# First pass of a convolution kernel: GpSimd works the taps of the fourth chunk, partial sums lie in PSUM, stores go to the sync queue

## The chip, the cores and the metric

The kernel runs on one core of one Trainium2 chip. The metric is the device time of one execution in microseconds. Three runs of the kernel before took 4022.09, 4029.52 and 4029.68 us, so the median is 4029.52. A separate execution was profiled; its own time is in the table below.

## The reference, cut to what matters

The input x is float32, 8 images of 512 channels of 128 x 128. Two branches are computed from it and joined. The part of the program at issue makes two things of x in one reading: a grouped convolution with stride 2 (two input channels to one output channel, 3 x 3 taps), and a projection of every channel's image onto 64 fixed cosine products.

```python
x = jax.lax.conv_general_dilated(sx, w_down, window_strides=(2, 2), padding=((1, 1), (1, 1)),
                                 feature_group_count=c2, dimension_numbers=('NCHW', 'OIHW', 'NCHW'))
...
xP = jnp.einsum('bcn,nk->bck', x2, P)
```

The convolution's result (8 x 256 x 64 x 64) feeds a k-means clustering, a mixture fit, a gate and a bilinear enlargement; the projection feeds an attention in the 64 coefficients. Both come back in a second pass over x. Those later passes are the same in both kernels.

## The kernel before

The program has a first pass, a cluster pass, an average pass, a mixture pass and a second pass, one after the other, with a barrier of all engines between them. Only the first pass is touched.

The first pass takes x in 16 groups: 8 images by T = 2 halves of the channels. A group is 128 partitions, each with the S = 2 input channels of one output channel. Each group is cut by rows into CH1 = 4 chunks of 32 rows. A chunk has one input buffer (`xt[c]`, 4.2 MB with one extra row above) and one accumulator (`acc[c]`, 128 x 16 x 64), so a buffer comes back into use once a group.

The convolution has 18 taps: two input channels by nine positions, each a strided window of the chunk times one weight per partition. For every chunk ScalarE writes tap 0 into the accumulator (L213) and counts `started`. VectorE adds the other 17 with one instruction each (L188): x window times weight plus accumulator, back into the accumulator. It takes chunks 0 and 1 together, one tap of each in turn, then 2 and 3. Each tap waits for the tap before it on the same chunk, by `tapped`. When a pair is done it counts `chunk_free` for each chunk. GpSimd issues the store of each accumulator to the array `downsampled` in HBM (L163), waits for it to land and counts `stored`, which ScalarE needs before it starts the same chunk of the next group.

The projection runs beside this. TensorE transposes x in quads, four 128 x 128 blocks at a time, into one of SLOTS = 4 PSUM banks (`first_tp`, L243); ScalarE copies a quad to SBUF (`first_xT`, L217); TensorE multiplies it into `first_freq` (L255) two quads behind the transposes. A group is 64 quads, 16 a chunk. At a group's end ScalarE copies the sums out (L220), TensorE folds the two halves (`first_sum`, L273) and ScalarE copies the result (L222).

The sync engine issues the loads of x in the order of chunks (L144). A load waits until TensorE has transposed the old contents (`pe_read`) and VectorE has done its taps (`chunk_free`).

The order of the work is written out by hand: each engine has its own list of instructions in a loop over images (SP and GpSimd over groups), with two groups in the loop's body, and semaphores join the lists. Engines run their lists strictly in order.

## Time and profile before

| | before |
|---|---|
| median of 3 runs | 4029.52 us |
| profiled execution | 4018.82 us |
| its span | 4017.1 us |
| first pass ends (first read of the cluster pass issued) | 1368.14 us |
| TensorE busy in the span | 3405.0 us (85%) |
| VectorE busy | 2899.9 us (72%) |
| ScalarE busy | 2079.5 us (52%) |
| GpSimd busy | 34.8 us (1%) |
| taps on VectorE, L188 | 1088, 1298.0 us busy, mean 1274 ns |
| transposes, L243, and products, L255 | 4096 each, 680.2 and 667.8 us busy |

The span runs from the first to the last instruction of the profiled execution. Busy time is the time in which an engine had at least one instruction under way; instructions overlap at their ends, so the mean of one tap (1274 ns) is more than the distance between two. PE is TensorE, PEld its weight loads, DVE VectorE, ACT ScalarE, POOL GpSimd, SP the sync engine, and a q behind an engine's name its queue. "Idle before" is how long the engine stood still before a row, and behind the arrow is what ended it; "issue" means that nothing the profile shows was waited for.

### The profile page before, as it was taken

The numbers are of one execution on the slowest core, as the hardware profiler recorded it, in microseconds if no ns is written. First come the engines' busy times: TensorE is split into PE (matmuls) and PEld (weight loads), VectorE is DVE, ScalarE is ACT, GpSimd is POOL, SyncE is SP. The second block draws the span as 40 slices with busy tenths as digits, with TensorE's granted clock in tenths as the row PEclk, the third lists the DMA queues.
The fourth block names the chain that finished last, engine by engine and source line by source line (L and its number), as shares of the span: only waits on it lengthen the run. The fifth ranks groups of instructions, "written<-read, shape, count | busy, mean of one in ns | idle before, by whom it ended". The sixth has DMA issues, their size and how long they took to land. (4 is left out here: it accounts for less than half of the span.)

```text
span 4017.1 us, 69326 instructions
## 1 busy us (share of the span) xinstructions
PE 3405.0 (85%) x24688; PEld 2542.9 (63%) x24688; DVE 2899.9 (72%) x3732; ACT 2079.5 (52%) x3496; POOL 34.8 (1%) x69
## 2 busy tenths in 40 slices
PE   7998999999999368995666898888888888888887
PEld 4454544545545266773444787878778787877877
DVE  5999999999999721114334877768677777868766
ACT  4555555555555202221112667666666666666766
POOL 0000000000000000000000000000000000000000
PEclk9999999999999668997887999999999999999999
DMA  6555565646565204210002999999899999989998
GB/s 282 227 236 246 220 262 204 267 205 261 220 246 237 81 0 167 108 70 0 0 0 91 345 316 320 318 321 323 305 333 322 330 318 322 324 314 330 315 348 284
DMA packets 348928, 945.65 MB, mean 235 GB/s; under 512 B 25938, under 2 KB 58834, under 8 KB 329491
## 3 DMA queue, kind: packets, MB, share of 16 engines
q1 hardware_dynamic: 339346, 907.41, 60.9%
q0 software_dynamic: 9216, 33.56, 2.1%
q8 instruction: 207, 3.39, 0.3%
q14 instruction: 159, 1.29, 0.1%
HBM read 638.89 MB, written 301.99 MB: 234 GB/s over the span
## 5 line engine op out<-in xcount | busy, mean ns | idle before, releaser
L188 DVE SCALAR_TENSOR_TENSOR first_acc<-first_x,first_wd,first_acc 128x1024 f32<-128x1024 f32 (+1 forms) x1088 | 1298.0, 1274 | 57.7 <-ACT first_acc L213 46.3
L1139 PE MATMUL second_o<-second_right,second_left 128*128 128x128 f32 x8192 | 1144.6, 285 | 105.6 <-ACT second_right L1220 61.9
L1139 PEld LDWEIGHTS second_o<-second_right,second_left 128*128 128x128 f32 x8192 | 1033.6, 198 | 162.0 <-issue 139.5
L1370 DVE TENSOR_TENSOR second_x<-second_o,second_x 128x512 f32<-128x512 f32 x1024 | 702.5, 689 | 465.3 <-PE second_o L1139 456.5
L217 ACT ACTIVATE first_xT<-first_tp 128x512 f32<-128x512 f32 x1024 | 609.2, 598 | 535.1 <-PE first_tp L243 534.7
L243 PE MATMUL first_tp<-all_const,first_x 128*128 128x128 f32 x4096 | 680.2, 291 | 78.7 <-issue 42.6
L243 PEld LDWEIGHTS first_tp<-all_const,first_x 128*128 128x128 f32 x4096 | 442.8, 144 | 461.0 <-issue 446.5
L255 PE MATMUL first_freq<-first_xT,all_p 128*64 128x256 f32 x4096 | 667.8, 407 | 17.5 <-ACT first_xT L217 7.8
L1192 ACT ACTIVATE second_scaled<-second_mid,second_shift,second_gain 128x512 f32<-128x512 f32 x512 | 388.6, 806 | 366.7 <-DVE second_mid L1352 338.4
L1215 ACT ACTIVATE second_left<-second_tp 64x512 f32<-64x512 f32 x512 | 302.5, 591 | 157.8 <-PE second_tp L1126 139.0
L1126 PE MATMUL second_tp<-all_const,second_scaled 128*128 128x128 f32 x2048 | 322.4, 282 | 29.1 <-ACT second_scaled L1192 29.1
L255 PEld LDWEIGHTS first_freq<-first_xT,all_p 128*64 128x64 f32 x4096 | 210.6, 136 | 193.4 <-issue 178.4
L1216 ACT ACTIVATE second_left<-second_tp 64x512 f32<-64x512 f32 x512 | 303.4, 593 | 5.9
L1126 PEld LDWEIGHTS second_tp<-all_const,second_scaled 128*128 128x128 f32 x2048 | 246.0, 145 | 44.2 <-ACT second_scaled L1192 36.2
L564 DVE TENSOR_TENSOR gates_ft<-gates_ft,average_mean 128x512 f32<-128x512 f32 x64 | 44.0, 688 | 239.8 <-PE average_mean L516 239.8
L1126 PE MATMUL second_tp<-all_const,second_zt 128*128 128x128 f32 x512 | 106.5, 291 | 121.7 <-ACT second_left L1216 121.6
L1340 DVE TENSOR_TENSOR second_part<-second_dd,all_inter 128x512 f32<-128x512 f32 x256 | 174.5, 682 | 0.0
L1340 DVE TENSOR_TENSOR second_mid<-second_dd,all_inter 128x512 f32<-128x512 f32 x256 | 174.3, 681 | 0.2 <-DVE second_rr L1321 0.2
L539 ACT ACTIVATE average_dT<-average_tp 128x512 f32<-128x512 f32 x128 | 74.9, 597 | 168.9 <-PE average_tp L494 168.9
L1352 DVE TENSOR_TENSOR second_mid<-second_mid,second_part 128x1024 f32<-128x1024 f32 x128 | 156.6, 1224 | 4.8 <-DVE second_rr L1321 1.6
L1126 PEld LDWEIGHTS second_tp<-all_const,second_zt 128*128 128x128 f32 x512 | 60.4, 144 | 139.8 <-ACT second_left L1216 137.4
L1069 PE MATMUL second_st<-second_pk,all_p 128*64 128x64 f32 x2048 | 142.8, 234 | 3.7 <-DVE second_pk L1275 3.7
(208 smaller groups left out, 2322.6 us busy)
## 6 DMA issues: line engine op xcount, KB each, us to landing
second_x<-in_x SPq DMA_DIRECT2D x512, 512.0 KB, 6.0
out<-second_x SPq DMA_DIRECT2D x512, 512.0 KB, 4.4
first_x<-in_x SPq DMA_DIRECT2D x48, 4224.0 KB, 25.3
first_x<-in_x SPq DMA_DIRECT2D x16, 4096.0 KB
second_dd<-downsampled SPq DMA_DIRECT2D x112, 384.0 KB, 5.7
downsampled<-first_acc POOLq DMA_DIRECT2D x64, 512.0 KB, 11.6
average_xd<-downsampled SPq DMA_DIRECT2D x16, 2048.0 KB, 8.6
second_dd<-downsampled SPq DMA_DIRECT2D x16, 320.0 KB, 5.5
```

What stands on the lines that cost most here:

```text
L188: nc.vector.scalar_tensor_tensor(out=acc[c][:, :, left:], in0=tap_window(xt[c], (s, dh, dw), OUT1), scalar=wd[:, t, k:k + 1], in1=acc[c][: ...
L217: nc.scalar.activation(xT[slot][:, :, :], tp[slot][:, :, :], ACT.Copy).then_inc(copied[slot], 1)
L243: last = nc.tensor.transpose(tp[slot][:, n * S + s, :], xt[c][:, s, 1 + r + n, :], ident)
L255: last = nc.tensor.matmul(freq_ps[t][n * UV:(n + 1) * UV, 0:S * P], p_sb[:, row, :], xT[slot][:, n * S:(n + 1) * S, :].rearrange("p s g -> ...
L1126: last = nc.tensor.transpose(tp[slot][:, i, :], src.rearrange("p h w -> p (h w)"), k("ident"))
L1139: last = nc.tensor.matmul(ob[n][:, r, :], left[a][:, r, n, :], right[a][:, r, :], start=True, stop=True)
L1192: last = nc.scalar.activation(scaled_rows[c][:, t, s, :, :], mid[c][:, t, :, :], ACT.Identity, scale=gain[:, n:n + 1], bias=shift[:, n:n + 1])
L1215: nc.scalar.activation(left[a][lo, 2 * n + 1, :, :], tp[slot][lo, :, :], ACT.Copy)
L1216: nc.scalar.activation(left[a][hi, 2 * n, :, :], tp[slot][hi, :, :], ACT.Copy).then_inc(copied[slot], 1)
L1340: last = nc.vector.tensor_tensor((mid[c], part)[r][:, :, :, :].rearrange("p t (i e) w -> p t i e w", e=2)[:, :, :, 1 - e, :], dd[c][:, :, ...
L1352: nc.vector.tensor_tensor(mid[c][:, :, :, :], mid[c][:, :, :, :], part[:, :, :, :], ALU.add).then_inc(interpolated, 1)
L1370: nc.vector.tensor_tensor(xt[i][:, n // S, n % S, :, :], ob[n][:, :, :], xt[i][:, n // S, n % S, :, :], ALU.add).then_inc(added[n], 1)
```

## The change

GpSimd takes the 17 taps of chunk 3 of each group. It has no instruction here that multiplies and adds at once, so each tap is a scaling into a buffer `product` and an add of it into the accumulator, both in SBUF; its list is written out for all 16 groups, without a loop. Each of the 34 instructions waits for the one before it. VectorE keeps chunks 1 and 0, one tap of each in turn, and then chunk 2 in two halves of 8 output rows, one tap of each half in turn. Its running sums lie in PSUM (`partial`): the first tap reads ScalarE's accumulator from SBUF, the last one writes it there. The order of the taps is new, so that the last covers all columns.

The two partial sums take four PSUM banks. The transposes therefore have two banks (TP_BANKS) where they had four, and the folded sums go to the free columns of `first_freq`. TensorE's transposes of quad q now wait for the copy of quad q - 2 in place of q - 4. The stores leave GpSimd and stand on the sync queue, each in front of the load of the same chunk of the next group. A load waits for `pe_read`; that the taps are done follows from the store before it, which waits for them.

On the sync engine, the loop over groups reads as follows before (`first_x` is a chunk's input, `downsampled` the array of results):

```order
L144 ISA [waits first_chunk_free2,first_pe_read2]
L144 DMA first_x<-in_x 128x2x4224
L144 ISA [waits first_chunk_free3,first_pe_read3]
L144 DMA first_x<-in_x 128x2x4224
L152 REGISTER_ALU
L152 COMPARE_AND_BRANCH
```

and now:

```order
L163 ISA [waits first_tapped2]
L163 DMA downsampled<-first_acc 128x1024
L151 ISA [waits first_pe_read2]
L151 DMA first_x<-in_x 128x2x4224
L163 ISA [waits first_tapped3]
L163 DMA downsampled<-first_acc 128x1024
L151 ISA [waits first_pe_read3]
L151 DMA first_x<-in_x 128x2x4224
L167 REGISTER_ALU
L167 COMPARE_AND_BRANCH
```

Before each load there is now a wait for the chunk's last tap and a store. On GpSimd the list of a group before is stores and waits:

```order
L163 ISA [waits first_tapped0]
L163 DMA downsampled<-first_acc 128x1024
L165 ISA
L163 ISA [waits first_xd_out0,first_tapped1]
L163 DMA downsampled<-first_acc 128x1024
```

and now (`first_product` is the scaled window, `first_wd` the weights):

```order
L190 TENSOR_SCALAR first_product<-first_x,first_wd 128x1024 [waits first_started,first_x_in3]
L194 TENSOR_TENSOR first_acc<-first_acc,first_product 128x1024 [waits first_tapped3]
L190 TENSOR_SCALAR first_product<-first_x,first_wd 128x1024 [waits first_tapped3]
L194 TENSOR_TENSOR first_acc<-first_acc,first_product 128x1024 [waits first_tapped3]
...
L190 TENSOR_SCALAR first_product<-first_x,first_wd 128x1024 [waits first_tapped3,first_started,first_x_in3]
```

The DMAs are gone from it; two arithmetic instructions a tap have come, every one with a wait for `tapped3`, and the next group's first one waits for ScalarE's start and the load as well. On TensorE the head of a group before is:

```order
L243 MATMUL first_tp<-all_const,first_x 128x128 [waits first_copied0]
L243 MATMUL first_tp<-all_const,first_x 128x128 x3
L243 MATMUL first_tp<-all_const,first_x 128x128 [waits first_copied1]
L243 MATMUL first_tp<-all_const,first_x 128x128 x3
L243 MATMUL first_tp<-all_const,first_x 128x128 [waits first_copied2]
L243 MATMUL first_tp<-all_const,first_x 128x128 x3
L251 REGISTER_ALU
L252 REGISTER_ALU [waits first_freq_read]
L255 MATMUL first_freq<-first_xT,all_p 64x256 [waits first_copied0]
```

and now:

```order
L290 MATMUL first_tp<-all_const,first_x 128x128 [waits first_copied2]
L290 MATMUL first_tp<-all_const,first_x 128x128 x3
L290 MATMUL first_tp<-all_const,first_x 128x128 [waits first_copied3]
L290 MATMUL first_tp<-all_const,first_x 128x128 x3
L287 REGISTER_ALU
L290 MATMUL first_tp<-all_const,first_x 128x128 [waits first_copied0]
L290 MATMUL first_tp<-all_const,first_x 128x128 x3
L298 REGISTER_ALU
L302 MATMUL first_freq<-first_xT,all_p 64x256 [waits first_copied0,first_freq_read]
```

Before, the three first quads waited for copies of the group before; now the third waits for the copy of this group's own first quad, as the first product does.

```diff
-TAPS = [(s, dh, dw) for dw in (0, 1) for dh in (-1, 0, 1) for s in range(S)] + \
-       [(s, dh, -1) for dh in (-1, 0, 1) for s in range(S)]
+TAPS = [(s, dh, dw) for dw in (0, -1, 1) for dh in (-1, 0, 1) for s in range(S)]
+TP_BANKS = 2
+POOL_CHUNK = 3
+STEPS = [TAPS_LEFT, TAPS_LEFT, 2 * TAPS_LEFT, 2 * TAPS_LEFT]
...
-        tp = [sc.ps(f"tp{i}", [P, 4, P]) for i in range(SLOTS)]
+        tp = [sc.ps(f"tp{i}", [P, 4, P]) for i in range(TP_BANKS)]
-        sum_ps = sc.ps("sum", [P, 512])
+        sum_ps = [bank[:, S * P:S * P + S * UV] for bank in freq_ps]
+        product = sc.sb("product", [P, OUT1, WD])
+        partial = [sc.ps(f"partial{i}", [P, OUT1, WD]) for i in range(2)]
...
                     sp.wait_ge(pe_read[c], i + FREE)
-                    sp.wait_ge(chunk_free[c], i + FREE)
...
+                def store(i, c):
+                    sp.wait_ge(tapped[c], i * STEPS[c] + STEPS[c] + FREE)
+                    sp.dma_start(xd.rearrange("b t g n -> (b t) g n")[i, :, c * OUT1 * WD:(c + 1) * OUT1 * WD],
+                                 acc[c][:, :, :].rearrange("g h w -> g (h w)")).then_inc(stored[c], 16)
+                with sp.Fori(0, B * T - 1) as i:
                     for c in range(CH1):
-                        load(i, c)
+                        store(i, c)
+                        load(i + 1, c)
...
             def _(pool):
...
+                for i in range(B * T):
+                    done = i * STEPS[c] + FREE
+                    pool.wait_ge(x_in[c], i * 16 + 16)
+                    pool.wait_ge(started, i * CH1 + c + 1)
+                    for n, (s, dh, dw) in enumerate(TAPS[1:]):
+                        left = 1 if dw < 0 else 0
+                        if n > 0 or i > 0:
+                            pool.wait_ge(tapped[c], done + 2 * n)
+                        nc.gpsimd.tensor_scalar(product[:, :, left:], tap_window(xt[c], (s, dh, dw), OUT1),
+                                                wd[:, i % T, weight_of(s, dh, dw)], None, ALU.mult
+                                                ).then_inc(tapped[c], 1)
+                        pool.wait_ge(tapped[c], done + 2 * n + 1)
+                        nc.gpsimd.tensor_tensor(acc[c][:, :, left:], acc[c][:, :, left:], product[:, :, left:],
+                                                ALU.add).then_inc(tapped[c], 1)
...
             def _(dve):
...
+                    before = acc[c] if n == 0 else mine
+                    after = acc[c] if n == TAPS_LEFT - 1 else mine
+                    return nc.vector.scalar_tensor_tensor(
+                        out=after[:, rows, left:], in0=tap_window(xt[c], (s, dh, dw), count, row0),
+                        scalar=wd[:, t, weight_of(s, dh, dw)], in1=before[:, rows, left:],
+                        op0=ALU.mult, op1=ALU.add)
...
+                        for n in range(TAPS_LEFT):
+                            for c in (1, 0):
...
+                                tap(t, c, n, slice(0, OUT1), partial[c]).then_inc(tapped[c], 1)
+                        c, half = 2, OUT1 // 2
+                        for n in range(TAPS_LEFT):
+                            for h in range(2):
...
+                                tap(t, c, n, slice(h * half, (h + 1) * half), partial[0]).then_inc(tapped[c], 1)
...
-                            pe.wait_ge(copied[slot], i * (quads // SLOTS) + q // SLOTS + FREE)
+                            before = (q - TP_BANKS) % SLOTS
+                            pe.wait_ge(copied[before], i * (quads // SLOTS) + (q - TP_BANKS) // SLOTS + 1 + FREE)
```

## Rows read from the trace of the kernel before

**Rows 1.** Timeline, all engines, end of the pass: start us, us, engine, line, work.

```profile
1355.17 0.53 POOL L163 DMA_DIRECT2D downsampled<-first_acc  x1 [36.44 <-DVE first_acc L188]
1358.78 0.53 POOL L163 DMA_DIRECT2D downsampled<-first_acc  x1 [3.08 <-DMA downsampled<-first_acc]
...
1368.14 0.82 SPq L313 DMA_DIRECT2D cluster_xx<-downsampled  x2
```

**Rows 2.** Stretch 100 to 1300 us: PE, PEld, DVE, ACT, POOL busy, clock, DMA, GB/s.

```profile
100.00:1300.00 1200.00, 1122.63 (x7560) 605.02 (x7558) 1187.35 (x996) 639.75 (x1033) 30.92 (x58) 0.97 0.58 237
```

**Rows 3.** Timeline of VectorE, two blocks of a group and the last block.

```profile
85.50 40.55 DVE L188 SCALAR_TENSOR_TENSOR first_acc<-first_x,first_wd,first_acc 128x1024 f32<-128x1024 f32 x34 [0.67 <-DVE first_acc L188]
126.40 40.55 DVE L188 SCALAR_TENSOR_TENSOR first_acc<-first_x,first_wd,first_acc 128x1024 f32<-128x1024 f32 x34 [0.34 <-DVE first_acc L188]
...
1315.15 40.55 DVE L188 SCALAR_TENSOR_TENSOR first_acc<-first_x,first_wd,first_acc 128x1024 f32<-128x1024 f32 x34 [0.23 <-DVE first_acc L188]
```

**Rows 4.** Timeline of ScalarE, starts of accumulators.

```profile
82.05 1.26 ACT L213 ACTIVATE first_acc<-first_x,first_wd 128x1024 f32<-128x1024 f32 x1
...
632.22 1.26 ACT L213 ACTIVATE first_acc<-first_x,first_wd 128x1024 f32<-128x1024 f32 x1 [1.64 <-DMA first_x<-in_x]
652.49 1.26 ACT L213 ACTIVATE first_acc<-first_x,first_wd 128x1024 f32<-128x1024 f32 x1
...
719.77 1.25 ACT L213 ACTIVATE first_acc<-first_x,first_wd 128x1024 f32<-128x1024 f32 x1
738.69 1.25 ACT L213 ACTIVATE first_acc<-first_x,first_wd 128x1024 f32<-128x1024 f32 x1
...
815.62 1.25 ACT L213 ACTIVATE first_acc<-first_x,first_wd 128x1024 f32<-128x1024 f32 x1
...
900.41 1.26 ACT L213 ACTIVATE first_acc<-first_x,first_wd 128x1024 f32<-128x1024 f32 x1
...
921.91 1.29 ACT L213 ACTIVATE first_acc<-first_x,first_wd 128x1024 f32<-128x1024 f32 x1
939.53 1.27 ACT L213 ACTIVATE first_acc<-first_x,first_wd 128x1024 f32<-128x1024 f32 x1
...
1308.86 1.27 ACT L213 ACTIVATE first_acc<-first_x,first_wd 128x1024 f32<-128x1024 f32 x1
```

**Rows 5.** Timeline of TensorE, heads of two groups and a wait for x.

```profile
514.42 2.82 PE L243 MATMUL first_tp<-all_const,first_x 128*128 128x128 f32 x12 [6.13 <-issue]
...
593.47 1.48 PE L243 MATMUL first_tp<-all_const,first_x 128*128 128x128 f32 x12
595.76 0.65 PE L255 MATMUL first_freq<-first_xT,all_p 128*64 128x256 f32 x4 [0.81 <-ACT first_xT L217]
...
632.24 0.66 PE L243 MATMUL first_tp<-all_const,first_x 128*128 128x128 f32 x4 [1.50 <-DMA first_x<-in_x]
...
633.67 1.12 PE L243 MATMUL first_tp<-all_const,first_x 128*128 128x128 f32 x4
```

**Rows 6.** The page's groups by line: out<-in xcount, busy, mean ns, idle before.

```profile
L1370 DVE TENSOR_TENSOR second_x<-second_o,second_x 128x512 f32<-128x512 f32 x1024 | 702.5, 689 | 465.3 <-PE second_o L1139 456.5
...
L1340 DVE TENSOR_TENSOR second_part<-second_dd,all_inter 128x512 f32<-128x512 f32 x256 | 174.5, 682 | 0.0
```

**Rows 7.** Groups of GpSimd, shapes apart.

```profile
L158 POOL MEMSET first_x<- 128x256 f32 x1 | 0.3, 312 | 0.3 <-POOLq L1514 0.3
L1514 POOL MEMSET const-float32-0.0<- 128x1 f32 x1 | 0.1, 99 | 0.4 <-issue 0.4
```

**Rows 8.** Line L144, loads of x issued from 120 to 130 us: ns, starts; landing.

```profile
L144 SPq DMA_DIRECT2D first_x<-in_x x2: 543/543/543, 125.1 to 126.3; - x2
...
DMA to landing us min/median/max: 15.3/20.3/25.4
```

**Rows 9.** Two short stretches, columns as in rows 2.

```profile
631.00:637.00 6.00, 4.76 (x24) 2.54 (x24) 6.00 (x6) 2.55 (x4) 0.00 (x0) 0.72 0.99 421
640.00:646.00 6.00, 6.00 (x43) 3.11 (x41) 6.00 (x6) 2.99 (x5) 0.00 (x0) 1.00 0.29 122
```

More of the change, by code:

```diff
@@ L170, in _, with tap @@
                 dve.wait_ge(top_zero, 1)
[L171 removed]
+                start_free(dve, tapped[:3])
+                def tap(t, c, n, rows, mine):
+                    s, dh, dw = TAPS[1 + n]
+                    left = 1 if dw < 0 else 0
+                    row0, count = rows.start, rows.stop - rows.start
+                    before = acc[c] if n == 0 else mine
[4 more added lines that the diff above has]
+                        op0=ALU.mult, op1=ALU.add)
```

69 lines of the change are left out of this document (31 added, 38 removed).

## The prediction

> **What bounds the kernel now.** I read the busy shares first, then a table of stretches, then the groups by line, then the order of time on VectorE, ScalarE and TensorE side by side, and last the DMA landings.
>
> The first pass ends at 1368.14, where the cluster pass issues its first read [rows 1]; nothing behind that point is touched, so the question is how far it moves. Between 100 and 1300 us VectorE is busy for 1187.35 of 1200 us, TensorE for 1122.63, GpSimd for 30.92 [rows 2]. That looks like one bound, VectorE, with a neighbour 6% behind. The order of time shows less distance. VectorE's taps run in blocks of 34 in 40.55 us, 1.193 us each, with 0.2 to 0.7 us between blocks [rows 3]: about 81.6 us for a group of four chunks. ScalarE starts the accumulator of each chunk in step with TensorE, so its rows show TensorE's pace [rows 4]: chunk 3 of the first group starts at 82.05, of the sixteenth at 1308.86, so 15 intervals of 81.8 us. A pair of groups, which is one turn of the loop, takes 163.6. Now take a stretch where no row has a wait for a DMA: chunk 3 starts at 738.69, 815.62 and 900.41, which is 76.9 us inside a pair and 84.8 across a loop end, together 161.7. The 84.8 holds a 6.13 us issue gap of TensorE at the head of its loop body, and 12 transposes in 2.82 us behind it, where the same 12 take 1.48 elsewhere [rows 5]. TensorE's own pace is therefore only 1.9 us a pair shorter than what is run today. VectorE and TensorE are bounds of nearly the same height. Unloading VectorE alone can give back about 8 x 1.9 = 15 us.
>
> **The change part by part.**
>
> VectorE. It keeps 34 full taps and 34 half taps of 68 full ones. Full: 34 x 1.193 = 40.6 us. Half: a two-input operation of 512 columns reads 682 ns [rows 6], one of 1024 columns 1274, of which 1193 count; 512 columns then count some 0.60 us, and 34 x 0.60 = 20.4. Sum 61.0 against 81.1, far below TensorE's 81. A partial sum in PSUM as input costs little by the rows: 689 ns where one input is PSUM, 682 where both are SBUF [rows 6]. No row has VectorE writing PSUM; I bound it by 0 and by 0.08 us (the whole tail of a tap, 1.274 long against 1.193 apart) and take 0.03.
>
> The Trainium skill (Perfetto Trace Analysis, "Optimizing Scalar/DVE Operations") puts the access overhead of VectorE at about 60 ns on SBUF and 125 ns on PSUM; by that estimate a tap is 0.065 us longer. No run here shows it.
>
> GpSimd. It gets 17 pairs of a scaling and an add, 34 instructions of 128x1024, each waiting for the one before, as GpSimd's rows in the section on the change show. The trace has no GpSimd arithmetic at all. The nearest rows are its memsets: 312 ns for 256 elements, 99 ns for one [rows 7], so 0.835 ns an element for one stream and 0.1 us fixed. If an instruction's streams all run beside each other, each costs 0.95 us, a pair 1.9. If they run one behind the other, the scaling (one in, one out) costs 1.81 and the add (two in, one out) 2.66, a pair 4.5. The handover from one instruction to its dependent is bounded by 0 and 0.34 us, VectorE's idle time between two blocks of a group, where it waits for its own result [rows 3]. So 17 taps take L = 32 us at least and 17 x (4.47 + 0.68) = 88 at most. Neither row is nearer than the other; I take the middle for the arithmetic, 3.19, and 0.28 for each of two handovers: 3.75 a tap, L = 63.8.
>
> The Trainium skill (GPSIMD Engine Reference, "Performance versus the Vector engine") gives 4497 ns for an fp32 add of 2048 elements; half of it with a one-input scaling at line rate would put L at an estimated 64, and its warning that ordinary elementwise work belongs on VectorE is the rule that speaks against this change. No run here shows either figure.
>
> The loop that L closes. Chunk 3 of a group can't start on GpSimd before ScalarE has started its accumulator, which ScalarE reaches only after the three chunks before it; and the x buffer of chunk 3 is reloaded only after the last add, since the store comes first on the sync queue and waits for it, as the queue's rows show there. From that add to the next start: 0.2 us to the issue (a chunk's last tap ends at 124.9, 1.2 before the block's end at 126.05 [rows 3]; the load goes at 125.1 [rows 8]), 0.6 for the store's own issue, 15.3 to landing [rows 8], 1.4 for the store that is ahead in the queue (the two loads, issued at 125.1 and 126.3, take 15.3 and 25.4, so they land 11.3 us apart, for 4.2 MB; the store is 0.5 MB), 1.3 for ScalarE's accumulator [rows 4]. Sum 18.8. The cycle is L + 18.8 = 82.6 us.
>
> TensorE with two transpose banks. Today it runs three quads of transposes at a group's head, 12 in a row, and its first product waits until 595.76 for the copy, which stands behind ScalarE's accumulator [rows 5]. Afterwards the third quad waits for that copy too (TensorE's rows there), so one quad of transposes (0.58 us) comes behind it: +0.6 inside a pair, +1.0 behind the loop end, where the clock is low. Inside a group a copy has about 1 us of slack to the transposes that need its bank, and the accumulator at a chunk's head (1.27) leaves some 0.3 of it, so I cost it at nothing there.
>
> The clock. After a wait of 1.5 us for x at 632.24, four matmuls take 1.12 us where they took 0.66 [rows 5]; the granted clock is 0.72 over 631 to 637 and 1.00 over 640 to 646 [rows 9], so the engine falls from 2.4 to 1.2 GHz for a while. A wait above 1.5 us for x costs some 1.3 us more: chunk 2 started at 632.22 and chunk 3 at 652.49, 20.27 apart, where 18.92 is usual, as 719.77 to 738.69 [rows 4]. I add 1.3 once for each such wait.
>
> Stores. They leave GpSimd's queue, where their issue and waits cost nothing today, since nothing waits for them. On the sync queue they stand ahead of the loads; the price, 0.6 + 1.4 us, is in the 18.8.
>
> **The sum.** Starts of chunk 3: 15 intervals, 8 inside a pair, 7 across. Inside, max(82.6, 76.9 + 0.6) = 82.6. Across, max(82.6, 84.8 + 1.0 + 1.3) = 87.1. From 82.05 [rows 4]: 82.05 + 8 x 82.6 + 7 x 87.1 = 1352.6, where it is 1308.86 today: +43.7. Then the tail. Today VectorE ends at 1355.70 and the next pass starts 12.4 us later, behind two stores in turn [rows 1, 3]. Afterwards GpSimd ends last, at 1352.6 + 1.3 + 63.8 = 1417.7; one store and the barrier follow, which take 9.4 today (1358.78 to 1368.14). The pass ends at 1427.1 instead of 1368.1: +59. The profiled execution took 4018.82 with a span of 4017.1; that gives 4078. The median of the three runs is 4029.52, 10.7 above the profiled one, so for a median I forecast 4088, 1.5% slower. Less than 0.2% (8 us) can't be told from no change.
>
> **Rivals.**
>
> A, GpSimd is quicker than the cycle needs (L below 59). Then TensorE sets the pace: 8 x 77.5 + 7 x 85.8 brings the last start to 1302.7, 6 us earlier than today, and the tail grows by L - 45.6 less 3. At L = 55 that is no change (about 4029), at 59 about +6. What takes the place of GpSimd is chunk 0: VectorE may begin only when ScalarE has started chunk 1 (921.91 to 939.53 and 1.3 more [rows 4], 18.9 us into the group), works 40.6, and the load lands 17.5 later: 77.0, against 77.5 when TensorE wants it. 0.03 a tap uses that up; 0.08 a tap makes 8 stalls of 2.2 + 1.3 us, +28: 4057. For it: one-input work may be quick. Against it: 34 dependent handovers.
>
> B, the other side: GpSimd's streams overlap fully, L is under 45, and taps into PSUM cost no more than today. Then TensorE's pace is reached and the tail shrinks: at L = 40 the pass ends at 1302.7 + 1.3 + 40 + 9.4 = 1353.4, -15: 4015. It decides from L = 47 down (0.2%). Only the lowest bound of the memset rows speaks for it.
>
> C, GpSimd is slower, L of 72 to 88. Each us above 68 costs 16: at 76, 15 x 94.8 + 82.05 + 1.3 + 76 + 9.4 = 1590.8, +223: 4252; at 88 +415. The serial sum of streams speaks for it. The Trainium skill (GPSIMD Engine Reference, "Performance pitfalls for Q7 kernels") has about 1.9 cycles an element even for reads of 8 bytes stride, as x is read here; with it L would be an estimated 77. No run here shows it.
>
> D, VectorE and GpSimd exclude each other at SBUF. In the rows VectorE works almost without a gap, so a GpSimd instruction would find it busy. If each waits for a VectorE tap, a pair takes 3.75 + 2 x 1.19 and L = 104.3; the cycle is 123.1 us, the pass ends at 2043.7, +676: 4705. The Trainium skill (SBUF — State Buffer, "Who interferes with whom") says that a VectorE instruction with two SBUF inputs excludes a GpSimd one that reads SBUF, and one with a single SBUF input does not; by it only the 4 first taps of a group would collide, a few us, and the partial sums in PSUM spare the rest.
>
> **Chances.** Forecast (L 59 to 71, slower by 10 to 150 us) 0.47; A 0.22, half of it within 0.2%; B 0.10; C 0.17; D 0.04. Faster 0.11, same 0.13, slower 0.76. The range takes in A, the near part of C and most of B's edge: 4018 to 4225. The forecast's own range is 4036 to 4172.
>
> **What would show it.** GpSimd's start-to-start time of a scaling and an add should be 3.75 us, near 1.7 and 2.1, and its block of 34 some 64 us. ScalarE's chunk-3 starts should lie 82.6 and 87 us apart by turns, with TensorE's wait for x at chunk 3 about 5 us inside a pair. VectorE should be busy for some 62 of 83 us, idle before each group. The first taps with two SBUF inputs may read longer. GpSimd's last add should be the last work of the pass, near 1418. The forecast is wrong if a pair of GpSimd instructions takes under 3.4 us (then A) or over 4.2 (then C), or if TensorE waits at chunk 0 rather than at chunk 3.

## The result, and the profile after

| | before | changed kernel |
|---|---|---|
| runs of the comparison, median | 4025.81 us (4 runs, 4014.71 to 4029.68) | 4516.1 us (4 runs, 4507.75 to 4520.85) |
| ratio | | 1.1206, 95% interval 1.1161 to 1.1251 |
| profiled execution | 4018.82 us, span 4017.1 | 4507.75 us, span 4506.0 |
| first pass ends | 1368.14 us | 1832.99 us |
| mixture pass, `mix_wc` to `second_dd` | 319.87 us | 349.33 us |

The changed kernel is 12% slower. The forecast was 4088 us, at most 4225: direction and mechanism were right, the size was not. Of the 488.9 us between the two profiled executions, 464.9 lie in the first pass. The mixture pass adds 29.5, the cluster and average passes 0.7, and the second pass gives 6.2 back; none of them was touched (the last experiment section returns to the mixture pass).

Where the pass ends, in the order of time of all engines (start us, us, engine, line, work, idle before and its releaser):

```profile
1821.50 2.34 POOL L194 TENSOR_TENSOR first_acc<-first_acc,first_product 128x1024 f32<-128x1024 f32 x1
1823.94 2.89 POOL L190 TENSOR_SCALAR first_product<-first_x,first_wd 128x1024 f32<-128x1024 f32 x1
1826.91 2.34 POOL L194 TENSOR_TENSOR first_acc<-first_acc,first_product 128x1024 f32<-128x1024 f32 x1
1829.27 0.33 SPq L163 DMA_DIRECT2D downsampled<-first_acc  x1
1832.99 0.81 SPq L360 DMA_DIRECT2D cluster_xx<-downsampled  x2
```

GpSimd's last add is the last work, as forecast, 412 us later than forecast. A tap takes 5.41 us here (add 1821.50 to add 1826.91), where VectorE is idle. Against [rows 1], the tail behind the last arithmetic has shrunk from two stores in turn to one: 3.7 us from the last add's end to the next pass.

The page's groups of the first pass (line, engine, work, count, busy us, mean ns of one, idle before and what ended it), which answer to [rows 6]:

```profile
L290 PE MATMUL first_tp<-all_const,first_x 128*128 128x128 f32 x4096 | 702.2, 297 | 477.7 <-DMA first_x<-in_x 394.1
L190 POOL TENSOR_SCALAR first_product<-first_x,first_wd 128x1024 f32<-128x1024 f32 (+1 forms) x272 | 805.1, 2960 | 351.9 <-ACT first_acc L259 326.7
L194 POOL TENSOR_TENSOR first_acc<-first_acc,first_product 128x1024 f32<-128x1024 f32 (+1 forms) x272 | 648.5, 2384 | 22.7
L209 DVE SCALAR_TENSOR_TENSOR first_partial<-first_x,first_wd,first_partial 128x1024 f32<-128x1024 f32 (+3 forms) x960 | 886.9, 1021 | 0.0
L209 DVE SCALAR_TENSOR_TENSOR first_partial<-first_x,first_wd,first_acc 128x1024 f32<-128x1024 f32 (+1 forms) x64 | 97.3, 1565 | 694.4 <-ACT first_acc L259 693.8
```

Two numbers carry the result. The scaling, with one tensor in and one out, takes 2960 ns, longer than the add with two in (2384). And TensorE, which waited 10.8 us for x between 100 and 1300 us before, has stood still for 394.1 us until loads of x landed, in 15 waits, each in front of chunk 3: one for each of the 15 groups after the first.

The stretches (PE, PEld, DVE, ACT and POOL busy with counts, granted clock, DMA share, GB/s), the first as in [rows 2], the second one cycle:

```profile
100.00:1300.00 1200.00, 856.84 (x5584) 457.52 (x5582) 726.95 (x766) 474.07 (x763) 989.20 (x371) 0.84 0.44 176
...
306.00:416.00 110.00, 77.74 (x518) 41.52 (x516) 69.97 (x76) 43.11 (x70) 90.84 (x35) 0.86 0.43 175
```

VectorE has fallen from 99% busy to 61%, TensorE from 94% to 71%, and GpSimd has risen from 3% to 82%. In a cycle of 110 us GpSimd is busy for 90.84. What is left of the cycle is the way from its last add to its next start. The 16 starts of these blocks lie 110.2 us apart on average (84.56 to 1737.44).

One turn of that loop, from the timelines of GpSimd, the sync queue and ScalarE:

```profile
503.50 2.90 POOL L190 TENSOR_SCALAR first_product<-first_x,first_wd 128x1024 f32<-128x1024 f32 x1
506.49 2.60 POOL L194 TENSOR_TENSOR first_acc<-first_acc,first_product 128x1024 f32<-128x1024 f32 x1
...
525.36 2.93 POOL L190 TENSOR_SCALAR first_product<-first_x,first_wd 128x1024 f32<-128x1024 f32 x1 [16.28 <-ACT first_acc L259]
```

```profile
509.25 0.34 SPq L163 DMA_DIRECT2D downsampled<-first_acc  x1
509.77 0.57 SPq L151 DMA_DIRECT2D first_x<-in_x  x1
```

```profile
523.97 1.23 ACT L259 ACTIVATE first_acc<-first_x,first_wd 128x1024 f32<-128x1024 f32 x1 [21.66 <-DMA first_x<-in_x]
```

The last add ends at 509.09. The store is issued 0.16 us later, the load at 509.77; it releases ScalarE at 523.97, 14.2 later; ScalarE's accumulator takes 1.23 and GpSimd starts at 525.36. TensorE stands before the same load:

```profile
523.99 1.12 PE L290 MATMUL first_tp<-all_const,first_x 128*128 128x128 f32 x4 [21.51 <-DMA first_x<-in_x]
525.03 1.12 PE L302 MATMUL first_freq<-first_xT,all_p 128*64 128x256 f32 x4
...
528.87 0.65 PE L302 MATMUL first_freq<-first_xT,all_p 128*64 128x256 f32 x4
```

```profile
510.00:524.00 14.00, 0.01 (x1) 0.01 (x1) 14.00 (x23) 0.03 (x1) 0.00 (x0) 0.50 0.99 370
524.00:528.00 4.00, 4.00 (x16) 2.01 (x16) 4.00 (x8) 2.40 (x3) 2.64 (x1) 0.50 1.07 417
532.00:545.00 13.00, 12.85 (x92) 6.99 (x92) 0.00 (x0) 6.58 (x11) 12.55 (x6) 1.00 1.02 419
```

After 21.51 us of standing still TensorE starts at a granted clock of 0.50, which is 1.2 GHz: four matmuls take 1.12 us for some 4 us, then 0.65 again at 2.4 GHz. This costs nothing here, because GpSimd sets the pace.

### The profile page after: what moved, and what is told of

It is laid out like the page before. It is cut to its first block and busy times, and to the rows that moved or that the text cites. A ratio compares the mean times of both kernels' runs of the same rounds, so it can differ in the third digit from the quotient of the medians.

```text
span 4506.0 us, 69894 instructions
## 1 busy us (share of the span) xinstructions
PE 3465.0 (77%) x24688; PEld 2561.7 (57%) x24688; DVE 2642.4 (59%) x3732; ACT 2081.2 (46%) x3496; POOL 1454.2 (32%) x549
## 5 line engine op out<-in xcount | busy, mean ns | idle before, releaser
L290 PE MATMUL first_tp<-all_const,first_x 128*128 128x128 f32 x4096 | 702.2, 297 | 477.7 <-DMA first_x<-in_x 394.1
L290 PEld LDWEIGHTS first_tp<-all_const,first_x 128*128 128x128 f32 x4096 | 453.6, 147 | 877.8 <-issue 457.5
L190 POOL TENSOR_SCALAR first_product<-first_x,first_wd 128x1024 f32<-128x1024 f32 (+1 forms) x272 | 805.1, 2960 | 351.9 <-ACT first_acc L259 326.7
L209 DVE SCALAR_TENSOR_TENSOR first_partial<-first_x,first_wd,first_partial 128x1024 f32<-128x1024 f32 (+3 forms) x960 | 886.9, 1021 | 0.0
L302 PE MATMUL first_freq<-first_xT,all_p 128*64 128x256 f32 x4096 | 684.0, 416 | 9.5
L194 POOL TENSOR_TENSOR first_acc<-first_acc,first_product 128x1024 f32<-128x1024 f32 (+1 forms) x272 | 648.5, 2384 | 22.7
L209 DVE SCALAR_TENSOR_TENSOR first_partial<-first_x,first_wd,first_acc 128x1024 f32<-128x1024 f32 (+1 forms) x64 | 97.3, 1565 | 694.4 <-ACT first_acc L259 693.8
L259 ACT ACTIVATE first_acc<-first_x,first_wd 128x1024 f32<-128x1024 f32 x64 | 79.2, 1237 | 396.4 <-DMA first_x<-in_x 396.3
## 6 DMA issues: line engine op xcount, KB each, us to landing
downsampled<-first_acc SPq DMA_DIRECT2D x64, 512.0 KB, 15.3
```

Of the source, the lines that this page charges most:

```text
L190: nc.gpsimd.tensor_scalar(product[:, :, left:], tap_window(xt[c], (s, dh, dw), OUT1), wd[:, i % T, weight_of(s, dh, dw)], None, ALU.mult). ...
L194: nc.gpsimd.tensor_tensor(acc[c][:, :, left:], acc[c][:, :, left:], product[:, :, left:], ALU.add).then_inc(tapped[c], 1)
L209: return nc.vector.scalar_tensor_tensor(out=after[:, rows, left:], in0=tap_window(xt[c], (s, dh, dw), count, row0), scalar=wd[:, t, weight ...
L290: last = nc.tensor.transpose(tp[q % TP_BANKS][:, n * S + s, :], xt[c][:, s, 1 + r + n, :], ident)
L302: last = nc.tensor.matmul(freq_ps[t][n * UV:(n + 1) * UV, 0:S * P], p_sb[:, row, :], xT[slot][:, n * S:(n + 1) * S, :].rearrange("p s g -> ...
```

## The experiments

Before was timed again beside the first four and the last four kernels: 4021.99 and 4021.43 us, medians of 23 runs each. The first pass's end is read from each profile, as the time at which the cluster pass issues its first read. Edits are to the changed kernel unless it is said otherwise.

### e1: all taps back on VectorE

```diff
-STEPS = [TAPS_LEFT, TAPS_LEFT, 2 * TAPS_LEFT, 2 * TAPS_LEFT]
+STEPS = [TAPS_LEFT, TAPS_LEFT, TAPS_LEFT, TAPS_LEFT]
...
-                        nc.gpsimd.tensor_scalar(product[:, :, left:], tap_window(xt[c], (s, dh, dw), OUT1),
...
-                            for c in (1, 0):
+                        for pair in ((1, 0), (3, 2)):
+                            for n in range(TAPS_LEFT):
+                                for c in pair:
```

The partial sums in PSUM, the two transpose banks and the stores on the sync queue stay.

> The changed kernel, but the taps of chunk 3 go back to VectorE (chunks 1 and 0, then 3 and 2, 68 full taps, sums in PSUM); GpSimd does none. Two transpose banks, PSUM sums and stores on the sync queue stay. Theory 'GpSimd's block closes the loop' (17 taps take 92 to 94 us, plus 16.2 us until the next block may start, 109.8 a group): all of the loss goes, VectorE's taps are 1.19 us apart, a group takes 81 to 83 us, the pass ends between 1360 and 1390, the time is 4020 to 4050. Rival 'the other three parts cost too': the time stays above 4080, with TensorE or VectorE slower per group.

Measured: 4040.25 us (12 runs), 1.0033 of before, interval 1.001 to 1.0055; the pass ends at 1378.35, 10.2 later than before. Of the 464.9 us of the pass, all but 10.2 therefore come with GpSimd's part. The 10.2 hold the two transpose banks (5.0 by e6) and the new order of chunks: between 100 and 1300 us VectorE now waits 34.6 us for ScalarE's accumulators, where it waited 2.1 before. The shares weren't separated further. VectorE's timeline shows what PSUM costs it:

```profile
1335.12 35.82 DVE L192 SCALAR_TENSOR_TENSOR first_partial<-first_x,first_wd,first_partial 128x1024 f32<-128x1024 f32 x30
```

30 taps with the running sum in PSUM are 1.194 us apart, where taps in SBUF were 1.193 [rows 3]. Each one lasts longer in the profile, 1401 ns on average for 1274, but the longer ends overlap with the next tap. In the profiled execution (4043.66) a further 14 us lie in the second pass, from `second_dd` to the end of the span: 1903.0 us against 1889.0. They are not explained.

### e2 and e3: 12 and 8 of the 17 taps on GpSimd

```diff
-                    for n, (s, dh, dw) in enumerate(TAPS[1:]):
+                    for n, (s, dh, dw) in enumerate(TAPS[1:13]):
```

Chunk 3 lacks 5 of its taps in e2, and 9 in e3 (`TAPS[1:9]`), so these kernels say what a shorter L would give.

> The changed kernel with only the first 12 of the 17 taps of chunk 3 on GpSimd; the other 5 are left out. Theory: 12 x 5.5 = 66 us, cycle 66 + 16.2 = 82.2, about the length that the prediction had assumed. Then the prediction's own sum can be tried: 82.2 inside a pair, 87.1 across, last start at 1350, pass ends 66 + 5 later at 1421, +53 against before, time about 4080. Rival 'only the cycle counts, TensorE's loop end adds nothing': 84.6 + 15 x 82.2 + 66 + 4 = 1388, time about 4047.

> The changed kernel with only the first 8 of the 17 taps of chunk 3 on GpSimd; the other 9 are left out. Theory: 44 us a block, cycle 60, far below TensorE's pace, so TensorE sets it: 77.5 inside a pair, 85.8 across, pass ends near 1352, 16 us before that of before: 4010, VectorE idle 20 us a group. Rival 'chunk 0 takes the place' (VectorE may start only with chunk 1, and the load of chunk 0 then comes late): TensorE waits for x at chunk 0, 2 to 4 us in each pair, time 4030 to 4050.

Measured, e2: 4111.89 us (4 runs), ratio 1.0187 (1.0129 to 1.0244), pass end 1429.90, where 4080 and 1421 were expected; the mixture pass has its longer form here (349.3 us), 29.5 more than in before's profile. With 12 x 5.5 = 66 us L and a way back of 16.2, the cycle stands where the forecast had put it (82.2 for 82.6), and the pass ends 61.8 us later than before; the forecast's sum said 59. Term by term the last start comes 7.4 us later than in that sum, the last block is 1.1 longer, and the tail is 5.7 shorter, so part of the agreement is luck. e3: 4038.22 us (12 runs), ratio 1.0016 (0.9986 to 1.0047), pass end 1358.43, 9.7 before the old one, where 4010 and 1352 were expected. The time lies in the range of the rival (4030 to 4050), but not for the rival's reason: with L = 44 TensorE doesn't wait for x any more, at chunk 0 or elsewhere, and the mixture pass has its longer form (351.9 us). The 9.7 us come from a shorter tail alone, since the last chunk 3 starts at 1309.49, before at 1308.86. Its waits in the profiles of e2 and e3 (engine, line, what for, us in total, times, longest):

```profile
PE first_tp L290 <- issue: 40.1, 7, 6.1
PE first_tp L290 <- DMA first_x<-in_x: 33.3, 9, 4.6
```

```profile
PE first_tp L290 <- issue: 41.0, 7, 5.9
PE first_tp L290 <- DMA all_p<-in_p_cols: 25.4, 1, 25.4
...
PE first_tp L290 <- ACT first_xT L263: 17.9, 15, 1.6
```

The 15 waits for x of the changed kernel, 394.1 us, are 9 waits of 33.3 us in all in e2 and none in e3. With them gone the groups come at TensorE's own pace: in e3 ScalarE starts chunk 3 at 81.93, 159.41 and 246.72, so 77.5 us apart inside a pair and 87.3 across. Over all 15 intervals it is 77.5 inside (79.0 twice) and 85.7 to 87.3 across, 86.4 on average. In e2, where a wait for x and a slow start of TensorE go before it, the interval across is 88.2 on average.

### e4: what in the scaling is slow

The scaling was written in six ways, turn by turn with n % 6. Other forms give other products. One execution was profiled.

```diff
+                        if n % 6 == 0:
+                            last = nc.gpsimd.tensor_scalar(out, window, weight, None, ALU.mult)
+                        elif n % 6 == 1:
+                            last = nc.gpsimd.tensor_scalar(out, window, 0.5, None, ALU.mult)
+                        elif n % 6 == 2:
+                            last = nc.gpsimd.tensor_scalar(out, xt[c][:, s, top:top + 31:2, left:WD], weight, None, ALU.mult)
+                        elif n % 6 == 3:
+                            last = nc.gpsimd.tensor_scalar(out, acc[c][:, :, left:], weight, None, ALU.mult)
+                        elif n % 6 == 4:
+                            last = nc.gpsimd.tensor_tensor(out, window, weight.unsqueeze(2).broadcast_to(
+                                [P, OUT1, WD - left]), ALU.mult)
+                        else:
+                            last = nc.gpsimd.tensor_copy(out, window)
```

> The changed kernel, where GpSimd's scaling takes six forms in turn over the taps (the sums come out wrong, as some forms read other data or another weight): as it is; with an immediate weight; with unit stride inside rows; wholly contiguous; as a two-input multiply with the weight broadcast; a plain copy of the window. As it is, it takes 2.95 us for 1024 elements, more than the two-input add with 2.38. Theory 'the stride of 8 bytes and the rows of x cost': the contiguous form falls to 1.6 us or less, the immediate one stays at 2.9. Rival 'the weight read per partition costs': the immediate form falls, the contiguous one stays. Second rival 'it is the operation itself': all scalings stay at 2.9 and the copy or the two-input multiply is quicker.

Measured: 4391.69 us, pass end 1715.87. The groups of GpSimd, each shape apart:

```profile
L208 POOL TENSOR_TENSOR first_acc<-first_acc,first_product 128x1024 f32<-128x1024 f32 x176 | 418.4, 2377 | 14.5
...
L194 POOL TENSOR_SCALAR first_product<-first_x,first_wd 128x1024 f32<-128x1024 f32 x32 | 94.0, 2936 | 327.4 <-ACT first_acc L273 325.8
L196 POOL TENSOR_SCALAR first_product<-first_x 128x1024 f32<-128x1024 f32 x32 | 92.4, 2889 | 3.0
L198 POOL TENSOR_SCALAR first_product<-first_x,first_wd 128x1024 f32<-128x1024 f32 x32 | 91.0, 2844 | 3.2
L200 POOL TENSOR_SCALAR first_product<-first_acc,first_wd 128x1024 f32<-128x1024 f32 x32 | 91.0, 2844 | 3.2
L202 POOL TENSOR_TENSOR first_product<-first_x,first_wd 128x1024 f32<-128x1024 f32 x32 | 61.1, 1909 | 2.5
...
L205 POOL COPY first_product<-first_x 128x1024 f32<-128x1024 f32 x16 | 19.4, 1210 | 1.0
```

Neither a constant in the instruction for the weight (L196, 2889 ns) nor rows of unit stride (L198) nor a contiguous input (L200, both 2844) takes more than some 3% off the 2936. A plain copy of the same strided window takes 1210. So the window's reading isn't what costs: TENSOR_SCALAR itself does, on GpSimd. The same product by TENSOR_TENSOR, with the weight broadcast as its second input (L202), takes 1909, a third less, although it has one more input.

### e5: the quicker form, and only part of the chunk

```diff
-TP_BANKS = 2
+TP_BANKS = 4
+VROWS = 6
...
-        partial = [sc.ps(f"partial{i}", [P, OUT1, WD]) for i in range(2)]
+        partial = [sc.ps(f"partial{i}", [P, OUT1 // 2, WD]) for i in range(2)]
...
+                        weight = wd[:, i % T, weight_of(s, dh, dw)].unsqueeze(2).broadcast_to([P, rows, WD - left])
+                        nc.gpsimd.tensor_tensor(product[:, VROWS:, left:], tap_window(xt[c], (s, dh, dw), rows, VROWS),
+                                                weight, ALU.mult).then_inc(pooled, 1)
```

GpSimd works 10 of the 16 output rows of chunk 3; VectorE works the other 6 and chunks 0 to 2, all in halves, with two sums of one PSUM bank each. Four transpose banks are free again. All of the computation is done.

> A version built from the findings. GpSimd takes 10 of the 16 output rows of chunk 3, its scaling is a two-input multiply with the weight broadcast (1.91 us for 1024 elements, where the scaling takes 2.94); VectorE takes the other 6 rows and chunks 0, 1, 2, all in two halves in turn, so that its sums need two PSUM banks only and the transposes have four again. Theory: GpSimd's tap costs 0.2 + 0.625 x 4.29 = 2.9 us, a block 49, cycle 65, no bound. VectorE 102 half taps at 0.655 and 34 of 192 elements at about 0.33: 78, with some us for first taps that wait for GpSimd. TensorE at its own pace, 161.7 a pair. The pass ends 13 to 20 us before that of before (1368): ratio 0.995 to 0.997. Rival 'VectorE stays the bound': half taps and collisions make 82 us and more a group, ratio 1.000 or above.

Measured: 4029.87 us (12 runs, 4008.95 to 4049.72), ratio 1.0014 (0.9985 to 1.0044); the pass ends at 1356.69, 11.4 us sooner than before. The groups of the two GpSimd instructions, and 30 of VectorE's short taps:

```profile
L198 POOL TENSOR_TENSOR first_acc<-first_acc,first_product 128x640 f32<-128x640 f32 x176 | 276.7, 1572 | 13.8
L195 POOL TENSOR_TENSOR first_product<-first_x,first_wd 128x640 f32<-128x640 f32 x176 | 224.8, 1277 | 540.6 <-ACT first_acc L251 528.0
```

```profile
1342.49 9.79 DVE L212 SCALAR_TENSOR_TENSOR first_partial<-first_x,first_wd,first_partial 128x192 f32<-128x192 f32 x30
```

The stretch from 100 to 1300 us, and what TensorE waits for x in this kernel:

```profile
100.00:1300.00 1200.00, 1137.22 (x7656) 611.55 (x7656) 1177.46 (x1958) 645.35 (x1047) 717.06 (x503) 0.97 0.59 232
```

```profile
PE first_tp L282 <- DMA first_x<-in_x: 4.0, 2, 2.3
```

A pair is 2.93 us, L is 51, and the loop no longer sets the pace. But the pass wins 11.4 us, where 13 to 20 were expected. GpSimd's 10 rows take 17 x 1.193 x 10/16 = 12.7 us a group off VectorE, but chunks 0 to 2 in halves cost 2 x 0.66 us a tap for 1.193, 51 x 0.127 = 6.5 us more a group, and the 6 rows in two parts 34 x 0.326 = 11.1 for 7.6, so most of it is spent again: VectorE is still busy for 1177.46 of the 1200 us. What sets the pace now is TensorE. It waits only 4.0 us for x, and ScalarE's starts of chunk 3 lie 76.9 us apart in 6 of the 8 intervals inside a pair, which is TensorE's own pace with four banks. The last one comes at 1295.48, 13.4 us sooner than before; the tail behind it is 1.9 longer. So the rival, VectorE as the bound, isn't what the starts show, although the ratio is the one that it gave.

The ratio of all runs cannot show the gain: the profiled execution (4037.59) has its mixture pass at 352.2 us, 32 longer than before's. The twelve times fall into two groups, and so do before's. The six short ones have a median of 4015.7 us, the 20 short ones of before beside them 4020.0, so about 4 us of the gain may be seen there; the split into groups was made after the fact.

### e6: the kernel before, with two transpose banks alone

```diff
-        tp = [sc.ps(f"tp{i}", [P, 4, P]) for i in range(SLOTS)]
+        tp = [sc.ps(f"tp{i}", [P, 4, P]) for i in range(TP_BANKS)]
```

with TensorE's waits as in the change; all else is the kernel before.

> The kernel before with two transpose banks for four, and nothing else. Theory 'two banks cost TensorE its lead': in the run with 8 taps TensorE waited for nothing but copies and still took 164.8 us a pair, against 161.7 with four banks; so here the pair grows from 163.6 to some 165, the pass ends 8 to 12 us later, ratio 1.002 to 1.003. Rival 'VectorE hides it': the pass ends within 3 us of 1368, ratio 1.000.

Measured: 4022.81 us (12 runs), ratio 1.001 (0.9977 to 1.0042), pass end 1373.18, 5.0 later. That is between the 8 to 12 us of the theory and the 3 us of the rival, and the total tells nothing. In the waits TensorE stands for the copy of `first_xT` at the head of a group:

```profile
PE first_tp L245 <- ACT first_xT L218: 16.4, 15, 1.3
```

The forecast had +0.6 inside a pair and +1.0 across; the waits are 1.1 us on average, and part of them took the place of a wait that the first product had before [rows 5]. Of some 16 us of waits, 5.0 reach the pass's end.

### e7: the load of chunk 3 issued before its store

```diff
-                        store(i, c)
-                        load(i + 1, c)
+                        if c == POOL_CHUNK:
+                            sp.wait_ge(tapped[c], i * STEPS[c] + STEPS[c] + FREE)
+                            load(i + 1, c)
+                            store(i, c)
+                        else:
+                            store(i, c)
+                            load(i + 1, c)
```

> The changed kernel, but for chunk 3 the sync queue issues the load of the next group ahead of the store. Theory: the load is on the loop that bounds the pass, GpSimd's last add to its next start, so the loop falls from 109.8 us by the store's issue (0.5) and its share of the transfer (1.1 to 1.4): 108 us, 15 intervals, 25 to 30 us, ratio to before 1.113 to 1.115 where it was 1.1206. Rival 'not on the loop, VectorE or TensorE set it': no change.

Measured: 4541.31 us (4 runs), ratio 1.1268 (1.1208 to 1.1328), pass end 1860.69: 27.7 us later than in the changed kernel, where a gain was expected. The expectation missed in sign. ScalarE and GpSimd at the same turn of the loop:

```profile
531.34 1.25 ACT L266 ACTIVATE first_acc<-first_x,first_wd 128x1024 f32<-128x1024 f32 x1 [25.24 <-DMA downsampled<-first_acc]
```

```profile
532.74 2.92 POOL L197 TENSOR_SCALAR first_product<-first_x,first_wd 128x1024 f32<-128x1024 f32 x1 [18.25 <-ACT first_acc L266]
```

ScalarE's new accumulator overwrites what the store reads, so it waits for load and store. With the store in front the load ended that wait; now the store, issued behind 4.2 MB of x, does: the load releases TensorE at 528.60 and the store ScalarE at 531.34. GpSimd's idle time at this turn grows from 16.28 to 18.25 us, and over the 15 turns from 243.1 to 270.6, 27.5 more, against the 27.7 measured. It was the wrong order to try, but it shows that each microsecond of the loop counts 15 times.

### e8: VectorE's sums in SBUF

```diff
-                    before = acc[c] if n == 0 else mine
-                    after = acc[c] if n == TAPS_LEFT - 1 else mine
+                    before = after = acc[c]
```

Each VectorE tap now reads two inputs from SBUF.

> The changed kernel with VectorE's running sums in the accumulators in SBUF instead of PSUM, so that each of its taps has two SBUF inputs. Theory 'two such inputs and GpSimd exclude each other': in the changed kernel the first taps, with two, take 1.79 us where the others take 1.31, up to 3.4. Here every tap collides: each GpSimd instruction waits for a tap and each tap for an instruction while both work; GpSimd's block grows from 94 us towards 150 and the time by 15 times that, to 5100 to 5400. Rival 'no exclusion': within 1% of 4516.

Measured, in one execution: 4809.11 us, pass end 2127.17, 294 later than the changed kernel, though less than the 5100 to 5400 expected: GpSimd's block grows from 94 to 113 us on average, not towards 150. GpSimd's timeline, first beside VectorE taps of 1024 columns, then beside taps of 512; below it VectorE's taps from 530 to 560 us and its block of half taps:

```profile
546.02 3.82 POOL L190 TENSOR_SCALAR first_product<-first_x,first_wd 128x1024 f32<-128x1024 f32 x1
549.92 2.66 POOL L194 TENSOR_TENSOR first_acc<-first_acc,first_product 128x1024 f32<-128x1024 f32 x1
...
601.53 18.74 POOL L190 TENSOR_SCALAR first_product<-first_x,first_wd 128x1024 f32<-128x1024 f32 x1 [16.10 <-ACT first_acc L258]
620.35 2.35 POOL L194 TENSOR_TENSOR first_acc<-first_acc,first_product 128x1024 f32<-128x1024 f32 x1
622.80 2.92 POOL L190 TENSOR_SCALAR first_product<-first_x,first_wd 128x1024 f32<-128x1024 f32 x1
```

```profile
529.17 31.08 DVE L208 SCALAR_TENSOR_TENSOR first_acc<-first_x,first_wd,first_acc 128x1024 f32<-128x1024 f32 x14
...
594.92 22.51 DVE L208 SCALAR_TENSOR_TENSOR first_acc<-first_x,first_wd,first_acc 128x512 f32<-128x512 f32 x34
```

Beside full taps both engines are slowed: the scaling takes 3.82 in place of 2.92, and VectorE's taps are 31.08 / 14 = 2.22 us apart in place of 1.19. Beside half taps one scaling lasts 18.74 us, from 601.53 to 620.27. VectorE's block of 34 is over at 617.43, 2.84 before that, about the length of one scaling, and VectorE keeps its 0.66 us a tap. The collision of rival D is real, though beside full taps it costs less than D's price; PSUM sums are what keeps it out of the changed kernel.

### What is left: the mixture pass

One stretch of the mixture pass, before and in the changed kernel:

```profile
1808.00:2128.00 320.00, 198.66 (x974) 128.16 (x974) 119.37 (x299) 48.80 (x79) 0.00 (x0) 0.82 0.00 0
```

```profile
2273.90:2623.20 349.30, 228.41 (x974) 140.30 (x974) 119.33 (x299) 48.80 (x79) 0.00 (x0) 0.71 0.00 0
```

The instructions are the same in number, VectorE's and ScalarE's busy times too; TensorE's granted clock is 0.71 for 0.82, and its part is 30 us slower. In the profiled executions the two forms go with the kernel: before, e1 and e6, without GpSimd's taps, have 319.9, 319.4 and 320.0 us; the changed kernel and e2, e3, e4, e5, e7 and e8, with them, have 349.3 to 352.2. The times without a profile suggest that both forms occur with and without these taps, if the groups into which they fall are the same two forms: five of before's 23 runs beside e1 lie at 4056 to 4064 us with a mean clock near 0.92, the others at 4015 to 4034 near 0.93; three of e6's twelve lie at 4050 to 4053 with 0.920 or 0.921; six of e5's twelve lie at 4009 to 4022 with 0.931 to 0.934, six at 4038 to 4050 with 0.921 to 0.923. All twelve of e3 have 0.920 to 0.924. So the long form doesn't need the change, but it is more frequent with it, and some of the change's 29.5 us may be its own cost. What decides between the forms was not tried and stays open.

## Why the prediction was right or wrong

**The mechanism held.** The loop was where it was put: GpSimd's last add, the store, the load of chunk 3, ScalarE's accumulator, GpSimd's first scaling. TensorE waits for x at chunk 3 in every group after the first, VectorE is idle before each group, and GpSimd's last add ends the pass. e1 shows that the rest of the change costs 10.2 us, so that the price lies with this loop.

**The step that failed is L, the 17 taps on GpSimd.** The forecast took 3.75 us for a pair, from 1.7 and 2.1, and 63.8 for 17. Measured: 2.99 from a scaling's start to its add's (503.50 to 506.49), a pair of 5.50, and 93.6 for 17 (195.57 to 289.15). That is above even the upper bound of 88, and a pair is past the 4.2 us that the forecast named as the sign for C. Of the 1.75 us that a pair is longer, 1.3 are the scaling and 0.4 the add. The bound was broken by one of its three parts: the add took 2.38 where 2.66 was the limit, the handover 0.09 where 0.34 was, but the scaling took 2.95 where 1.81 was. That 1.81 came from memsets [rows 7], by the assumption that an instruction costs what its streams cost one behind the other. e4 shows the assumption at fault: a copy, with the same two streams, takes 1.21, inside the bounds, and TENSOR_SCALAR 2.84 to 2.94 whatever its strides and its weight. Why this operation costs so much on GpSimd stays open, and whether some single GpSimd instruction could do a whole tap no run tried. A price that depends on the operation can't be bounded from rows of another operation. With no GpSimd arithmetic in the trace, 0.17 was too little for rival C, and the range's upper end of 4225 left out most of what C's own formula gave.

**From L to the end.** The cycle is 93.6 + 16.2 = 109.8 (the average over the pass is 110.2) where 82.6 was forecast. GpSimd's last start is at 1737.44 where 1353.9 was forecast, +383.5; the last block of 17 takes 91.8 for 63.8, +28.0; the tail 3.7 for 9.4, -5.7. Together 405.8, which with the 59 forecast makes the 464.9 of the pass. The form of the sum was sound, but two of its terms were too high: with the measured L of 93.6 and all else as forecast it gives 1872 for the 1833.0 measured. With the measured way back (16.2) and tail (3.7) as well it gives 1828; with these and the L of e2, 66 us, 1420 for the 1429.9 measured, and with the 44 us of e3 1352 for 1358.4.

**The way back, 18.8.** It is 16.2 us (289.15 to 305.33), 2.6 less, or 39 over 15 intervals: an error that hid part of the one in L. The load released ScalarE 14.2 us after its issue, where 15.3 and 1.4 for the store ahead were taken. The other order of store and load makes a turn 1.8 longer on average (e7).

**VectorE, 61.0 us a group.** It is busy for some 67 (726.95 of 1200 us at 110.2 a group). The full taps were right, 30 in 35.70 us, 1.19 apart; the half taps take 0.66, 30 in 19.73 us, where 0.60 was taken, and the first taps, shown below, add about 2 us a group. With 43 us idle in each group none of it counts:

```profile
468.02 35.70 DVE L209 SCALAR_TENSOR_TENSOR first_partial<-first_x,first_wd,first_partial 128x1024 f32<-128x1024 f32 x30
...
509.55 19.73 DVE L209 SCALAR_TENSOR_TENSOR first_partial<-first_x,first_wd,first_partial 128x512 f32<-128x512 f32 x30
```

The 0.03 us for PSUM was too much; e1 makes it 0.00 from tap to tap. The Trainium skill's (Perfetto Trace Analysis, "Optimizing Scalar/DVE Operations") higher overhead for PSUM, by which a tap would be 0.065 us longer, is not borne out for these taps: they are 1.194 us apart in PSUM and 1.193 in SBUF.

**TensorE's two banks.** Its own pace is 77.5 inside a pair (e3; forecast 77.5) and 86.4 across on average (forecast 85.8), 163.9 together, where the stretch with four banks gave 161.7. That is no less than the 163.6 of before, so the banks cost all that unloading VectorE could bring: e3's chunk 3 of the last group starts no sooner than before's, and e6 shows +5.0 in the pass with nothing unloaded.

**The clock.** After the wait shown the granted clock is 0.50 for some 4 us, the same fall as in [rows 5, 9]; it costs nothing while GpSimd sets the pace. In e2 such a wait costs time: behind a wait for x the interval across is 88.2 us, without one in e3 86.4. The forecast took 1.3 for these 1.8, and 87.1 for the 88.2. Seven times 1.1 is 7.7 of the 9.5 us by which e2's pass exceeds the sum with the measured way back and tail; how much of the 1.8 is clock was not separated.

**The rivals.** A and B needed L under 59 and 47: e3 shows that with L = 44 the pass would win 9.7 us and the total nothing that can be told (1.0016). Their last start at 1302.7 was 6.8 us too soon (1309.49 in e3). The stall at chunk 0 that A feared doesn't come. C is what happened, past its own end: its formula at L = 88 gave +415, the pass has +464.9. D's exclusion was kept out by the PSUM sums, as the Trainium skill's rule (SBUF — State Buffer, "Who interferes with whom") had it: a VectorE instruction with one SBUF input doesn't contend with GpSimd, one with two does. The trace agrees on both sides: beside taps with their sums in PSUM a scaling takes 2.95 us on average in the changed kernel, and 2.93 where VectorE is idle; beside full taps with two SBUF inputs it takes 3.82 in e8. The first taps, which read x and the accumulator from SBUF, take longer beside GpSimd than the later ones (each shape apart):

```profile
L209 DVE SCALAR_TENSOR_TENSOR first_partial<-first_x,first_wd,first_partial 128x1024 f32<-128x1024 f32 x288 | 347.1, 1308 | 0.0
...
L209 DVE SCALAR_TENSOR_TENSOR first_partial<-first_x,first_wd,first_acc 128x1024 f32<-128x1024 f32 x32 | 55.9, 1790 | 693.8 <-ACT first_acc L259 693.8
L209 DVE SCALAR_TENSOR_TENSOR first_partial<-first_x,first_wd,first_acc 128x512 f32<-128x512 f32 x32 | 41.4, 1339 | 0.6
```

1790 ns for 1308, on 32 taps, and 1339 for 746 on the halves: 34 us of VectorE's idle time in the whole pass, on nobody's path. Without GpSimd's arithmetic, in e1, the first taps take 1378 ns and the later ones 1401, so it isn't the SBUF input alone that makes them longer. With all taps of that kind, e8 pays 294 us.

**Outside the pass** the forecast left 0 and 24.0 came: 29.5 by the longer form of the mixture pass and 0.7 in the passes before it, less 6.2 in the second pass.

## What to carry to other kernels

Before work is moved to an engine that does none of it in the trace, measure one instruction of exactly that operation there: its cost depends on the operation, and here one operation took 2.95 us in place of the 1.81 that seemed the most. It made three quarters of the error of 30 us in a block, and an error in a block counts again in each of the 15 turns of the loop. An engine that holds a single-buffered tile puts its whole block, the reload and the next start in series, so ask first whether that sum is shorter than the present cycle; here it was 109.8 against 81.8. And an engine that is 99% busy is hardly worth unloading when its neighbour stands 1.9 us a pair behind it: e5, with four banks and a block of 51 us, won 11.4 us of the pass.

## What the runs showed of the hardware

- On GpSimd in float32, 128x1024: TENSOR_SCALAR 2.84 to 2.95 us, TENSOR_TENSOR add 2.38, TENSOR_TENSOR multiply with a broadcast second input 1.91, copy 1.21 (e4). An operation with one input was slower than the same product with two.
- From one GpSimd instruction to its dependent one: 0.09 us (503.50 + 2.90 to 506.49).
- VectorE's taps with a running sum in PSUM are as far apart as with one in SBUF: 1.194 us (e1) and 1.193 (before).
- A GpSimd scaling next to VectorE taps with two SBUF inputs: 3.82 us beside taps of 1024 columns, which were 2.22 us apart for 1.19; 18.74 beside taps of 512, which went on at 0.66 us each (e8). The shorter taps left GpSimd no turn in this stretch.
- A pass with the same instructions and the same busy times of VectorE and ScalarE took 320 or 349 to 352 us, with TensorE's granted clock at 0.82 or 0.71.
